# A message-passing kernel's dense tables built by groups of five nodes, in units of three edge tiles

## What is computed

```python
deg = segment_sum(ones_like(dst), dst, N)            # edges per target
segment_sum((x * norm)[src], dst, N) * norm          # layers 0 and 3: no edge weight
segment_sum(edge_weight[:, None] * h[cols], rows, N) # layer 2: with edge weight
```

## Time and profile before

| | before |
|---|---|
| median of 3 runs | 9939.35 us (9939.27 to 9943.32) |
| the profiled execution's own time | 9935.04 us |
| its span from first to last instruction | 9933.2 us |
| mean granted TensorE clock | 0.819 |
| busy over the span: PE, DVE, ACT, POOL | 76%, 42%, 25%, 19% |

### The profile page before, as it was taken

How to read it: one execution, slowest core, us unless ns; L and a number is a source line. 1 busy time by engine, 2 the same in 40 slices (tenths; PEclk the granted TensorE clock), 3 DMA queues, 4 the chain that set the end, 5 groups by cost and what they waited for, 6 DMA issues and landing times. The chain is left out here.

```text
span 9933.2 us, 193226 instructions
## 1 busy us (share of the span) xinstructions
PE 7507.0 (76%) x59876; PEld 5740.8 (58%) x59877; DVE 4212.0 (42%) x16253; ACT 2509.1 (25%) x14806; POOL 1929.9 (19%) x3544
## 2 busy tenths in 40 slices
PE   4988876555555555499885999999997993696285
PEld 3877765444444444388753888888884442343173
DVE  7988876544544544501122222222224006203714
ACT  0244445444544454200000111111111002001101
POOL 1111110000000000000001777777772000000000
PEclk9999998877877777699975777777776996897586
DMA  0011111111111111277732222222221990694062
GB/s 23 22 62 52 68 69 68 59 69 69 58 69 69 69 58 69 83 277 276 255 114 59 48 48 48 48 48 48 48 48 37 305 297 24 210 298 145 7 240 83
DMA packets 283195, 1005.48 MB, mean 101 GB/s; under 512 B 84845, under 2 KB 85997, under 8 KB 253613
## 3 DMA queue, kind: packets, MB, share of 16 engines
q1 hardware_dynamic: 232814, 952.06, 28.0%
q0 software_dynamic: 50176, 51.48, 2.8%
HBM read 749.76 MB, written 243.85 MB: 100 GB/s over the span
## 5 line engine op out<-in xcount | busy, mean ns | idle before, releaser
L1410 PEld LDWEIGHTS banks<-T 128*128 128x128 bf16 x31752 | 2237.8, 117 | 329.7 <-issue 90.2
L1410 PE MATMUL banks<-T 128*128 128x128 bf16 x31752 | 2386.7, 229 | 0.0
L1407 PE MATMUL banks<-T 128*128 128x512 bf16 x2646 | 1087.5, 411 | 1284.2 <-ACT ACC L1168 565.1
L547 POOL DMA_INDIRECT WORK<-table,idx x1568 | 1498.8, 956 | 596.5 <-issue 441.5
L743 DVE TENSOR_SCALAR T<-T 128x128 bf16<-128x128 bf16 x7956 | 1519.5, 247 | 0.0
L739 DVE TENSOR_SCALAR T<-T 128x128 bf16<-128x128 f16 x2652 | 661.3, 249 | 1460.7 <-PE banks L1410 1436.2
L1379 PE MATMUL banks<-T,WORK 128*128 128x250 bf16 x4900 | 1061.6, 272 | 64.2 <-DVE WORK L826 64.2
L1442 PE MATMUL banks<-T,WORK 128*64 128x392 f32 x3200 | 1062.8, 495 | 18.0 <-DMA T<-dense_w 11.0
L1380 PE MATMUL banks<-T,WORK 128*128 128x250 bf16 x4900 | 1061.3, 269 | 0.0
L1407 PEld LDWEIGHTS banks<-T 128*128 128x128 bf16 x2646 | 271.5, 103 | 1359.1 <-issue 812.7
L740 DVE TENSOR_SCALAR T<-T 128x512 bf16<-128x512 f16 x2652 | 918.5, 346 | 0.0
(11 more groups left out here) (277 smaller groups left out, 6339.9 us busy)
## 6 DMA issues: line engine op xcount, KB each, us to landing
T<-dense_w SPq DMA_DIRECT2D x400, 784.0 KB, 4.2
T<-dense_c SPq DMA_DIRECT2D x100, 1562.5 KB, 6.9
dense_w<-WORK SPq DMA_DIRECT2D x128, 1220.0 KB
T<-dense_c SPq DMA_DIRECT2D x100, 1500.0 KB, 7.0
WORK<-in_eaT SPq DMA_DIRECT2D x196, 256.0 KB
dense_c<-T SPq DMA_DIRECT2D x13, 3062.5 KB, 10.3
dense_c<-ACC SPq DMA_DIRECT2D x12, 3062.5 KB, 9.2
WORK<-table,idx POOLq DMA_INDIRECT x1568
```

Of the source, the lines that this page charges most:

```text
L547: nc.gpsimd.indirect_dma_start(out=g_sb[:, u, c * D:(c + 1) * D], out_offset=None, in_=table, in_offset=bass.IndirectOffsetOnAxis(ap=idx[: ...
L1407: T.matmul(banks[:, 2 + u, :], planes[:, v, 0, :], hot[:, v, :], start=begins and v == 0, stop=False, skip_group_check=True)
L1410: last = T.matmul(banks[:, u, j * P:(j + 1) * P], keys[:, j, :], planes[:, v, 1 + k, :], start=begins and v == 0 and j == 0 and k == 0, st ...
```

## The change

Only `ranges`, `build_dense` and the degree stage are changed. A group is now five targets (245 keys), so there are 1250 groups and SETS = 10; the sub-table of a group has two keys per partition instead of four. The run of tiles of a group is cut into units of three tiles, rounded up, and the number of units of a group is then made odd. DVE makes a whole unit with two instructions: one `is_equal` over 3 x 128 x 3 elements (two one-hot rows of the key, one of the low part, for three tiles, the tile number innermost) and one `mult` of the same size for the weight rows. There are SLOTS = 2 buffers, each for a unit. PE multiplies per tile once 245 columns for the counts and six times 128 or 129 columns for the weights; the 129th column is a column of ones, which adds up the degree of the keys. Four PSUM banks take turns, one for each group. With an odd number of units and four groups unrolled, buffer and bank are constants in PE's code. ACT copies a group with two instructions. SP stores a batch with three DMAs (112, 10 and 1 partitions) and doesn't wait for them; ACT waits for the stores of the batch before last.

The core of the diff:

```diff
-GROUP = 10
+GROUP = 5
 KEYS = GROUP * HI
-WIDE = 512
+WCOLS = P + 1
...
-SPAN = 8
+SPAN = 5
 BATCH = 5
-GROUPS = -(-NP // (GROUP * SPAN)) * SPAN
+GROUPS = NODES // GROUP
 SETS = -(-GROUPS // P)
 QUAD = 3
 QRING = 4
+SLOTS = 2
+TURN = 4
...
+        def bounds_of(eng, g, n):
+            return loads(eng, ranges_sb[0:1, 0, ds(g, n + 1)], 0, GROUPS * COLS)
...
-            def batch_out(n, u):
-                sp.wait_ge(group_copied, n * BATCH + (BATCH + 2))
+            def batch_out(n, slot):
+                sp.wait_ge(group_copied, n * BATCH + (BATCH + TURN))
                 batch = dense_w[ds(n * (BATCH * KEYS), BATCH * KEYS), :].rearrange("(b k) l -> b k l", b=BATCH)
-                full = KEYS // 4
-                sp.dma_start(batch[:, 0:full * 4, :].rearrange("b (m j) l -> m b (j l)", j=4), dense_out[0:full, u, :, :]).then_inc(batch_stored, 16)
-                sp.dma_start(batch[:, full * 4:KEYS, :].rearrange("(a b) k l -> a b (k l)", a=1),
-                             dense_out[full:full + 1, u, :, 0:(KEYS - full * 4) * P]).then_inc(batch_stored, 16)
-                sp.wait_ge(batch_stored, n * 32 + 32)
-                sp.sem_inc(batches_free, 1)
+                most, pairs = P // 16 * 14, KEYS // 2
+                for first, past in ((0, most), (most, pairs)):
+                    sp.dma_start(batch[:, 2 * first:2 * past, :].rearrange("b (m j) l -> m b (j l)", j=2),
+                                 dense_out[first:past, slot, :, 1:1 + 2 * P]).then_inc(batch_stored[slot], 16)
+                sp.dma_start(batch[:, 2 * pairs:KEYS, :].rearrange("b k l -> k b l"),
+                             dense_out[pairs:pairs + 1, slot, :, 1:1 + P]).then_inc(batch_stored[slot], 16)
...
-                nc.gpsimd.tensor_copy(quads[:, ds(slot, 1), 1:5, :].rearrange("p s k c -> p (s k) c"), lists[:, 1:5, ds(col, QUAD)])
-                nc.gpsimd.tensor_tensor(quads[:, ds(slot, 1), 0, :].rearrange("p s c -> p (s c)"), lists[:, 0, ds(col, QUAD)],
-                                        gbase[:, ds(g, 1)].to_broadcast([P, QUAD]), ALU.subtract).then_inc(quad_taken, 1)
+                nc.gpsimd.tensor_copy(quads[:, ds(slot, 1), 2:6, :].rearrange("p s k t -> p (s k) t"), lists[:, :, ds(col, QUAD)])
+                nc.gpsimd.tensor_tensor(quads[:, ds(slot, 1), 0:2, :].rearrange("p s k t -> p (s k) t"),
+                                        keyf[:, ds(col, QUAD)].unsqueeze(1).to_broadcast([P, 2, QUAD]),
+                                        gbase[:, :, ds(g, 1)].to_broadcast([P, 2, QUAD]), ALU.subtract).then_inc(quad_taken, 1)
...
+                fin(V.tensor_scalar(g_int, g_int, 1, None, ALU.bitwise_or))
...
-                        dve.wait_ge(quad_taken, now)
-            for v in range(QUAD):
-                            q_key, q_low, *q_w = (quads[:, s, k, v:v + 1] for k in range(5))
-                            dve.wait_ge(pair_free[v], now)
-                            V.tensor_scalar(planes[:, v, 0, :], iota_h[:, 0:P], q_low, None, ALU.is_equal).then_inc(low_ready[v], 1)
-                            last = V.tensor_scalar(hot[:, v, :], iota_h, q_key, None, ALU.is_equal)
-                            dve.wait_ge(low_ready[v], now)
-                            for k in range(3):
-                                last = V.tensor_scalar(planes[:, v, 1 + k, :], planes[:, v, 0, :], q_w[k], None, ALU.mult)
-                            last.then_inc(pair_ready[v], 1)
+                def hots(now, s):
+                    v = s % SLOTS
+                    dve.wait_ge(quad_taken, now)
+                    dve.wait_ge(pair_free, now)
+                    V.tensor_tensor(planes[:, v, 0:HOTS].rearrange("p (k n t) -> p k n t", k=3, t=QUAD),
+                                    iota2.unsqueeze(1).to_broadcast([P, 3, P, QUAD]),
+                                    quads[:, s, 0:3, :].unsqueeze(2).to_broadcast([P, 3, P, QUAD]), ALU.is_equal).then_inc(hots_ready, 1)
+                def weights(now, s):
+                    v = s % SLOTS
+                    dve.wait_ge(hots_ready, now)
+                    V.tensor_tensor(planes[:, v, HOTS:PLANES].rearrange("p (k n t) -> p k n t", k=3, t=QUAD)[:, :, 0:P, :],
+                                    planes[:, v, 2 * P * QUAD:3 * P * QUAD].rearrange("p (n t) -> p n t", t=QUAD).unsqueeze(1).to_broadcast([P, 3, P, QUAD]),
+                                    quads[:, s, 3:6, :].unsqueeze(2).to_broadcast([P, 3, P, QUAD]), ALU.mult).then_inc(pair_ready, 1)
...
-                    act.wait_ge(pair_free[QUAD - 1], past + 1)
-                    C.activation(dense_out[:, u // BATCH, b, :], banks[:, u % 2, :], ACT.Copy)
-                    for k in range(GROUP):
-                        keys = slice(k * HI, (k + 1) * HI)
-                        last = C.activation(counts_out[d // WAYS][:, :, d % WAYS + k], banks[:, 2 + u % 2, keys], ACT.Copy,
-                                            accum_out=row_sums[:, u * GROUP + k:u * GROUP + k + 1])
-                    last.then_inc(group_copied, 1)
+                        act.wait_ge(batch_stored[b0], turn * (48 * BATCHES) + (j // 2 + 1) * 48)
...
+                    act.wait_ge(pair_free, bounds[b + 1] + SLOTS)
+                    bank = (j * BATCH + b) % TURN
+                    C.activation(dense_out[:, b0, b, :], banks[:, bank, KEYS:KEYS + 2 * WCOLS], ACT.Copy)
+                    C.activation(counts_out[slot][:, :, d:d + GROUP], banks[:, bank, 0:KEYS].rearrange("p (h d) -> p h d", h=HI), ACT.Copy).then_inc(group_copied, 1)
...
+                def pair(now, v, u, begins):
+                    pe.wait_ge(pair_ready, now)
+                    hot = planes[:, v, 0:2 * P * QUAD].rearrange("p (n t) -> p t n", t=QUAD)
+                    keys = planes[:, v, 0:2 * P * QUAD].rearrange("p (m j t) -> p t j m", j=2, t=QUAD)
+                    lows = planes[:, v, 2 * P * QUAD:HOTS].rearrange("p (n t) -> p t n", t=QUAD)
+                    for t in range(QUAD):
+                        T.matmul(banks[:, u, 0:KEYS].rearrange("p (h d) -> p d h", h=HI), lows[:, t, :], hot[:, t, 0:KEYS].rearrange("p (d h) -> p d h", h=HI),
+                                 start=begins and t == 0, stop=False, skip_group_check=True)
+                for j in range(2):
                             for k in range(3):
...
+                                last = T.matmul(banks[:, u, to - low // QUAD:to + P + high // QUAD], keys[:, t, j, :],
+                                                planes[:, v, first - low:past + high].rearrange("p (n t) -> p t n", t=QUAD)[:, t, :],
+                                                start=False, stop=False, skip_group_check=True)
+                    last.then_inc(pair_free, 1)
...
+                        pair(begin + (1 + QRING), v, u, True)
+                        with pe.If(past > begin + 1):
+                            with pe.Fori(begin + 1, past, 2) as q:
+                                pair(q + (1 + QRING), 1 - v, u, False)
+                                pair(q + (2 + QRING), v, u, False)
...
-            for i in range(BLOCKS):
-                for c in HALVES:
-                    begin(pe, at_deg, i, c)
-                    did(times(A2[c], all_ones, lambda j: NORM_full[:, i * BLK + c * PUB + j * SUB:i * BLK + c * PUB + (j + 1) * SUB]), c)
+            for i in range(DEG_STEPS):
...
+                for n in range(GROUP):
+                for j in range(2):
+                        last = T.matmul(to[:, n, :], sel[:, n, j, :], degp[:, i * DEG_GROUPS:i * DEG_GROUPS + groups, j],
+                                        start=n == 0 and j == 0, stop=n == GROUP - 1 and j == 1, skip_group_check=True)
```

More of the change, by code:

```diff
@@ new lines, in gnn_kernel @@
+        low, wa, wb, wc = (lists[:, k, 0:COLS] for k in range(4))
+        gbase = T12[:, 4730:4730 + 2 * GROUPS].rearrange("p (k g) -> p k g", k=2)
+        iota2 = T12[:, 7230:7230 + QUAD * P // 2].bitcast(BF16).rearrange("p (n t) -> p n t", t=QUAD)
+        planes = T12[:, 7430:7430 + SLOTS * PLANES // 2].bitcast(BF16).rearrange("p (s n) -> p s n", s=SLOTS)
+        quads = T12[:, 10440:10440 + QRING * 6 * QUAD // 2].bitcast(BF16).rearrange("p (s k t) -> p s k t", s=QRING, k=6)
+        sel = T12[:, 11520:11520 + GROUP * 2 * D].rearrange("p (i j f) -> p i j f", i=GROUP, j=2)
@@ L318, in load, with loads, deltas_of @@
             return nc.s_assert_within(eng.value_load(of), low, high, skip_runtime_bounds_check_because="it was worked out within them")
-        def quads_of(eng, g, n):
-            bounds = ((0, GROUPS * COLS), (1, GROUPS * COLS), (-QUAD * GROUPS * COLS, COLS))
-            return [load(eng, ranges_sb[0:1, ds(g * 4 + k, 1)], bounds[k][0], bounds[k][1]) for k in range(n)]
+        def loads(eng, of, low, high):
+            _, values = nc.values_load_multi_w_load_instructions(of, engines=[eng.engine], min_val=low, max_val=high,
+                                                                 skip_runtime_bounds_check_because="they were worked out within them")
```

(20 more changed lines are left out.)

271 lines of the change are left out of this document (138 added, 133 removed).

## The result

The changed kernel takes 9310.39 us (median of 4 runs, 9309.14 to 9310.95), the kernel before 9941.33 (4 runs beside them). The ratio is 0.9365, 95% interval 0.9349 to 0.9381: 6.4% faster, 631 us. The forecast was 8540, 1400 us faster. The direction and the range hold, the size doesn't: less than half of the gain came.

What follows compares the result with a forecast made beforehand. PE and DVE were taken to bound the build up to about 1500 us, then the slow store. 9935 - 3984 + 53 - 11 + 10 + 12 = 6015, plus 1436 x 1.76 = 2527, gives 8540 us; range 8230 to 9420.

Steps and rivals of the forecast that it cites:

- The stores: Build's batch stores: 112 partitions spread over 16 engines take 3 us, so SP no longer waits and the second part's bound goes.
- The number of units: Build: groups of five give 1369 units, 1436 once each group's number is odd, against 882 quads before.
- The edges: Around the units: ranges +51 and DVE preparations +2, first DVE work 10, last stores 12, degree stage -11 us.
- PE's price: PE in the build: 3045 columns a unit at 0.432 ns a column, 1.31 us at the full clock.
- DVE's price: DVE in the build: 0.76 us per 1152-element instruction at two elements a cycle, 1.47 us a unit.
- The cycle of two buffers: Build: a buffer is filled, handed over (0.1), read by PE and free after 3.2 us, so 1.6 us a unit.
- The 10%: Build: allowance on the 1.6 us a unit, between the 5 and 12% over pace seen before, giving 1.76 us.
- The first rival: Build: something in a unit costs PE, POOL or ACT more, 2.0 to 2.6 us a unit, 8890 to 9750; chance 18%.
- if matmuls of 128 columns start further apart than 56 ns: PE in the build: one of the signs listed as showing the forecast wrong.
- the unit under 1.55 us: Build: case faster than the forecast's 1.55 to 2.0 us a unit, left outside the range of 8230 to 9420.

Runs made afterwards that it cites:

- e1: Kernel before with one edit, a batch's 122 partitions stored as transfers of 112 and 10 instead of one: 9342 us, ratio 0.8924.
- e6: Changed kernel with a batch's 122 partitions stored as one transfer again, not as 112 and 10: 10376 us, ratio 0.9916.
- e2: Changed kernel with the weight matmuls' moving rows read side by side instead of in steps of three (other values): 9441 us, ratio 0.9015.
- e7: Changed kernel with the weight matmuls' moving rows side by side and DVE's innermost runs of four elements instead of three (other values): 9277 us, ratio 0.8879.
- e10: Changed kernel with all moving and stationary operands and counts PSUM columns side by side, DVE's runs of four (other values): 9148 us, ratio 0.8743.
- e3: Changed kernel with stationary operands read side by side instead of in steps of six and three (other values): 9821 us, ratio 0.9379.
- e5: Changed kernel with the counts matmul writing PSUM side by side instead of in steps of five, ACT reordering: 9774 us, ratio 0.9336.
- e8: Changed kernel with a tile's first three weight matmuls reading moving rows in steps of two, the last three of four (other values): 9844 us, ratio 0.9421.
- e11: Changed kernel with units of two tiles instead of three and a ring of eight instead of four quads between POOL and DVE: 9311 us, ratio 0.8900.
- e12: Changed kernel with units of two tiles, a ring of eight, and POOL loading bounds for ten groups instead of five: 9156 us, ratio 0.8737.

## Why the prediction was wrong in size

- **The stores** went as forecast: spread, no long issue, ACT's wait gone. This edit alone gives more than the whole gain (e1), and without it the rest of the change gains 0.8% (e6).
- **The number of units** was right: 1436 of L785.
- **The edges** were right. Start of the build +54.9 us (188.9 - 134.0; forecast +53); from the last start of L785 to the degree stage 17 us (forecast 12 behind the last unit); the degree stage 54.7 against 68.1 us, -13.4 (forecast -11); from there to the end 5754.7 against 5757.1. Outside the units the sum is off by a few us.
- **The step that failed is PE's price**, "A unit now is 3 x (245 + 4 x 128 + 2 x 129) = 3045 columns, 1.31 us at the full clock". It took the 0.432 ns a column of a kernel whose moving operands lie side by side, and used it for rows in steps of three. A unit needs 2.25 us and 0.04 at its end. (2.29 - 1.76) x 1436 = 761 us is nearly the whole miss of 770. Step by step the build falls from 3292 us to 2929 with the weight matmuls' moving rows side by side (e2), to 2725 with DVE's runs of four (e7), to 2597 with the other operands of PE side by side (e10); 70 us are left to the forecast's 2527.
- **DVE's price** failed too, under the cover of PE's: 0.97 instead of 0.76 us. "I take two [elements a cycle], since all operands are 2-byte and run along the innermost dimension in steps of one" is right about the mode, but the innermost dimension has three elements, and each run costs as much as one of four. With the weight matmuls near PE's price and DVE as it is, a unit takes 2.04 us (e2), and the first measurement would have been near 8950 us, an estimate (6015 + 1436 x 2.04).
- **The cycle of two buffers** was right: with the shapes for which the prices hold, 1.63 us a unit from 200 to 400 us (e10), though its 0.1 us for the handing over and 0.2 until PE's end is seen stood in no row. **The 10%** came out about right (1.76 to 1.85 us later on), in part by luck: POOL's stops for its registers, which the forecast doesn't name, grow in that stretch.
- **The first rival** is what happened, at 18%: a unit of 2.0 to 2.6 us. It named the steps in the stationary operands and in PSUM, and these are the two that cost least (21 and 53 us of build, e3 and e5). The moving operand, 363 us (e2), it did not name. The reason against it, that PE was busy for 75% only, was made with the very price in question. Of the signs that I gave, "if matmuls of 128 columns start further apart than 56 ns" was the one that came.
- Two slips on which nothing hung: the earlier trace rows lie at 3002 us, in the second part and not in the first (the pace at 500 us is the same, 0.91 us from L739 to L739), and the listed chances add up to 100% without the unit under 1.55 us that the range's 18% counts.
- The rounding up to odd numbers, 67 units by my count, is 153 us at 2.29 us; that wasn't tried by itself.

## What to carry to other kernels

Split a change into the edit that removes the bound and the rest, and price each against what is left: here the first gave 1.1 ms and the rest took half of it back. A layout that interleaves tiles so that VectorE can do them in one instruction is paid for on TensorE, which reads it in steps: price the moving operand's step before anything else. Here a run of two was the best that was tried: a run of three costs VectorE as much as one of four (e7), and a step of four costs TensorE still more than one of three (e8). An engine's share of busy time is no argument against a rival if it was worked out with the price that the rival doubts.

## What was not expected of the hardware

- Six matmuls with 770 moving bf16 columns: 0.36 us at a step of one (e2), 0.40 at two and 0.68 at four (e8, three matmuls each, counted twice), 0.56 at three, all at a granted clock of 1.00. A stationary step of six elements costs 22 ns a weight load (126 against 104), hidden beside the matmul.
- A PSUM output in steps of five fp32 costs a matmul of 245 columns some 0.02 us of 0.20 (e5).
- A bf16 tensor_tensor of 1152 elements: 0.96 us in runs of three, 0.76 in runs of four; 768 elements in runs of two 0.56. The three fit 0.16 us fixed, one cycle of 1.04 ns for a run of two and two for a run of three or four.
- POOL stands still for 3 to 13 us where it loads bounds for the next groups into registers; one load takes 0.57 to 5.5 us in e11 and up to 8.8 in e12. Why some take so long stays open; only their weight was shown (e12).
